# Attention output kept feature-major in a four-layer DiT stack: heads merged and sums gathered by DMA instead of TensorE transposes

## The chip, the cores and the metric

One Trainium2 chip, one core. The time is the device time of the kernel in microseconds (us), lower is better. TensorE is called PE, its weight loads PEld, VectorE DVE, ScalarE ACT, GpSimd POOL, and SyncE, whose queue issues most DMAs, SP.

## The reference

Sixteen sequences of 256 tokens with 256 features run through four layers, all in fp32. Of each attention block only this matters here (16 heads of 16 features):

```
def _attn(q, k, v):
    scores = jnp.einsum('bqhd,bkhd->bhqk', q, k) * scale
    w = jax.nn.softmax(scores, axis=-1)
    out = jnp.einsum('bhqk,bkhd->bqhd', w, v)
    return out.reshape(B, Lq, D_MODEL)
...
x = res + _attn(q, k, v) @ out_w          # self: 256 keys; cross: 77 context tokens
...
x = res + (gelu(xn @ ffn_w1.T + ffn_b1) @ ffn_w2.T + ffn_b2)
```

Layers L0, L2 and L3 are self attention, cross attention, MLP; L1 is cross attention alone. So a sequence passes 7 attention blocks and the kernel has 112 of them. L0's self attention also has a mask. Norms, modulation, gates, biases and rotary embedding differ from layer to layer and are not touched.

## The kernel before

A job is one sequence in one layer (64 jobs). Six jobs are in flight, each with its own slot of buffers. A job is cut into named steps, each on one engine. At build time a planner (`Program.run`) simulates the steps with a table of costs (`cost`), buffer rings and priorities, and writes down an order for each engine; at run time every engine goes through its own list in that order and waits on semaphores where a step's inputs or buffers are not there yet. So an engine whose next step must wait does nothing, even if a later step could run.

The steps of an attention block that are named below, with the line of their instructions:

- `qkv`: projections on PE (L1180, L1146). `ve` moves the values into `v_self` or `v_cross`, by ACT (L1426) or, where there is a bias, by DVE (L1617, L1625). There each head has 17 columns: its 16 features and a column of ones, so that the weighted sum also gives the softmax denominator.
- `S` (PE L1208 for self, L1222 for cross): a piece of the scores with queries in the partitions, written to one of two `score` banks. `mr` (DVE L1637) takes the row maxima out of that bank. `mx` (DVE L1650 to L1656) negates and turns them, and `sd` (SP, L1058) spreads them into `q_stack`. A self block has 8 `S`, a cross block 4.
- `ST` (PE L1238 for self, L1244 for cross): the same scores with keys in the partitions, less the maximum, into the same two banks. `ex` (ACT L1454) exponentiates them into `probs`.
- `W` (PE L1263): probabilities times values. Four heads sit in four 32-column tiles of the array. `pv` (ACT L1461) copies the sum of two `W` steps to `oT`: features of the heads in the partitions, tokens along the row. This is done in two halves of 8 heads.
- `oX` (PE L1274): four 128x128 transposes bring a half back to tokens in the partitions. `dv` (DVE L1665, L1666) inverts the sums and multiplies into `at`. `atT` (PE L1285): four transposes a block bring the result back to features in the partitions, `ae` (ACT L1466) copies it to `atT`, and `out` (PE L1146) projects it.

The MLP's steps are `up` (PE L1305), `ge` (ACT L1480) and `down` (PE L1314). The score steps use the array as row tiles of 64, `W` as column tiles of 32, all else as one tile.

## Time and profile before

| | |
|---|---|
| time, median of 3 runs | 2863.39 us (2859.39 to 2871.44) |
| profiled execution: first to last instruction | 2855.2 us |
| PE / DVE / ACT / POOL busy | 2716.6 / 1990.0 / 1433.3 / 290.6 us |
| mean granted TensorE clock | 0.973 of full |

The profiled execution has no other time of its own than its span, which is 8.2 us under the median of the runs and 4.2 us under the fastest; what lies around the span is in the runs' times. Busy time of PE counts each instruction from its first to its last moment, so neighbours overlap: what a group costs in a full stretch is read from the chain of waits, from its start to the next group's start. The layers lie one after another: L0 up to about 860 us, L1 to about 1200, then a passage, L2 from about 1400, L3 from about 1990 us.

### The profile page before, as it was taken

What the parts mean: (1) busy time and instruction counts of PE and PEld (TensorE: products, weight loads), DVE (VectorE), ACT (ScalarE), POOL (GpSimd) and SP (SyncE); (2) the same over time, 40 slices, a digit from 0 to 9 for tenths busy, and PEclk for the clock granted to TensorE, in tenths of its full rate; (3) what the DMA queues carried; (4) which work ended last, traced back from release to release, by engine and by line L of the source; (5) the groups of instructions that cost most, each with busy time, mean ns of one, the idle gap of its engine ahead of it and who ended that gap; (6) DMA issues with size and microseconds to landing.
All of it is one profiled execution on the core that took longest, in us unless ns stands there. A gap on an engine that the chain in (4) does not pass through costs nothing.

```text
span 2855.2 us, 57728 instructions
## 1 busy us (share of the span) xinstructions
PE 2716.6 (95%) x21118; PEld 2000.2 (70%) x21118; DVE 1990.0 (70%) x5348; ACT 1433.3 (50%) x2283; POOL 290.6 (10%) x346
## 2 busy tenths in 40 slices
PE   6989999999998999988999999999999999999998
PEld 5657777776766766665777777776777777676766
DVE  4677757766755577776777777776877777787751
ACT  1344554554455455444555555545555555555453
POOL 0000000000001111101111111110100000000000
PEclk9999999999999999997999999999999999999999
DMA  6443343343335366653434444434344433434320
GB/s 199 154 137 116 117 141 106 99 145 109 104 95 149 115 198 191 196 163 122 155 122 139 126 141 125 141 121 131 104 141 138 139 112 107 146 103 145 101 69 14
DMA packets 278894, 369.43 MB, mean 129 GB/s; under 512 B 31130, under 2 KB 157690, under 8 KB 278300
## 3 DMA queue, kind: packets, MB, share of 16 engines
q1 hardware_dynamic: 246172, 318.66, 36.8%
q10 hardware_dynamic: 32256, 47.07, 4.5%
q8 instruction: 177, 2.90, 0.4%
q14 instruction: 97, 0.79, 0.1%
q0 software_dynamic: 192, 0.01, 0.0%
HBM read 224.52 MB, written 110.97 MB: 118 GB/s over the span
## 4 chain that ended last, share of the span: by engine, by line
PE 70%; DVE 16%; issue 5%; DMA 4%; ACT 1%; SPq 1%; POOL 0%; ACTq 0%; DVEq 0%; POOLq 0%
PE gen L1305 11%; PE gen L1314 11%; PE gen L1180 10%; PE gen L1146 8%; PE gen L1263 8%; DVE row_max L1637 6%; PE score L1238 3%; PE score L1193 3%; PE score L1208 3%; PE score L1244 2%; PE gen L1274 2%; PE gen L1155 2%; PE score L1222 2%; DMA parts_scratch<-parts 2%; DVE maxT L1656 2%
## 5 line engine op out<-in xcount | busy, mean ns | idle before, releaser
L1637 DVE TENSOR_REDUCE row_max<-score 128x4 f32<-128x1024 f32 (+1 forms) x640 | 652.6, 1044 | 107.9 <-PE score L1222 88.2
L1454 ACT ACTIVATE probs<-score 128x1024 f32<-128x1024 f32 (+1 forms) x576 | 566.2, 1022 | 268.2 <-PE score L1238 170.3
L1305 PE MATMUL gen<-xnT,w_w1M 128*128 128x256 f32 x1536 | 378.4, 394 | 4.7 <-ACT xnT L1396 2.6
L1314 PE MATMUL gen<-w_w2M,hT 128*128 128x256 f32 x1536 | 354.8, 385 | 8.6 <-DVE x L1688 5.7
L1490 POOL TENSOR_TENSOR rstd<-var_eps,minus_half 128x2 f32<-128x2 f32 x160 | 111.5, 697 | 2175.1 <-DVE var_eps L1533 2175.1
L1314 PEld LDWEIGHTS gen<-w_w2M,hT 128*128 128x128 f32 x1536 | 286.2, 191 | 59.2 <-issue 22.3
L1305 PEld LDWEIGHTS gen<-xnT,w_w1M 128*128 128x128 f32 x1536 | 286.1, 194 | 58.8 <-issue 4.9
L1480 ACT ACTIVATE hT<-gen,b_b 128x256 f32<-128x256 f32 x384 | 160.2, 471 | 166.6 <-PE gen L1305 165.7
L1396 ACT ACTIVATE xnT<-gen,mod_all 128x256 f32<-128x256 f32 x288 | 147.0, 564 | 181.0 <-PE gen L1155 164.4
L1656 DVE STREAM_TRANSPOSE maxT<-max_tok 32x64 f32<-32x64 f32 x896 | 208.9, 233 | 17.1
L1461 ACT COPY oT<-gen 128x512 f32<-128x512 f32 x224 | 131.6, 587 | 171.4 <-PE gen L1263 168.9
L1208 PE MATMUL score<-k_self,q_stack 64*128 64x256 f32 x1536 | 195.7, 343 | 19.7 <-DVE row_max L1637 17.3
L1263 PE MATMUL gen<-probs,v_self 128*17 128x256 f32 x3072 | 201.8, 383 | 0.3 <-ACT probs L1454 0.3
L1686 DVE TENSOR_TENSOR xhat<-gen,gate 128x256 f32<-128x256 f32 (+1 forms) x112 | 60.2, 537 | 203.2 <-PE gen L1314 147.8
L1208 PEld LDWEIGHTS score<-k_self,q_stack 64*128 64x128 f32 x1536 | 128.1, 190 | 95.9 <-issue 77.0
L1238 PE MATMUL score<-q_stack,k_self 64*128 64x256 f32 x1536 | 181.2, 334 | 2.9 <-ACT probs L1454 2.2
L1222 PEld LDWEIGHTS score<-k_cross,q_stack 64*128 64x128 f32 x2048 | 137.5, 192 | 50.6 <-issue 49.5
L1238 PEld LDWEIGHTS score<-q_stack,k_self 64*128 64x128 f32 x1536 | 122.1, 188 | 64.5 <-issue 46.0
L1222 PE MATMUL score<-k_cross,q_stack 64*128 64x78 f32 x2048 | 156.3, 284 | 9.1 <-DVE row_max L1637 5.8
L1263 PE MATMUL gen<-probs,v_cross 77*17 77x256 f32 x2048 | 159.7, 402 | 4.9 <-DVE xhat L1666 1.9
L1665 DVE RECIPROCAL row_max<-gen 128x16 f32<-128x16 f32 x224 | 55.0, 246 | 133.1 <-PE gen L1274 132.9
L1274 PE MATMUL gen<-ident,oT 128*128 128x128 f32 x896 | 143.2, 284 | 0.0
(162 smaller groups left out, 4166.4 us busy)
## 6 DMA issues: line engine op xcount, KB each, us to landing
q_stack<-parts_scratch SPq DMA_DIRECT2D x336, 256.0 KB, 3.8
parts_scratch<-parts ACTq DMA_DIRECT2D x160, 256.0 KB, 2.6
parts_scratch<-parts SPq DMA_DIRECT2D x160, 256.0 KB, 2.9
k_self<-parts_scratch SPq DMA_DIRECT2D x144, 256.0 KB, 4.0
q_stack<-zeros_scratch SPq DMA_DIRECT2D x112, 256.0 KB, 3.9
q_stack<-maxT SPq DMA_DIRECT2D x224, 128.0 KB, 2.6
k_cross<-parts_scratch SPq DMA_DIRECT2D x192, 78.0 KB, 2.5
x_scratch<-x SPq DMA_DIRECT2D x48, 256.0 KB, 3.1
```

Source lines behind the costliest of these rows:

```text
L1146: mm = pe.matmul(out, xT[:, fc], weight[:, fc, cols], start=fc == 0, stop=fc == FC - 1)
L1180: mm = pe.matmul(out[:, c, :], weight[:, fc, cols], xT[:, fc, :], start=fc == 0, stop=fc == FC - 1)
L1208: mm = pe.matmul(buf[:, t, c * S:c * S + S], queries[rows, column(u), c * P:c * P + P], keys[rows, column(u), :], start=not blk.mask, stop ...
L1222: mm = pe.matmul(buf[:, t, at_col:at_col + CTXP], queries[rows, column(2 * u + i), c * P:c * P + P], keys[rows, column(2 * u + i), :], sta ...
L1238: mm = pe.matmul(buf[:, t, kc * S:kc * S + S], keys[rows, column(u), kc * P:kc * P + P], queries[rows, column(u), :], start=not blk.mask, ...
L1263: mm = pe.matmul(pv[VW * i:VW * i + VC, within, :], value, e, start=kc == 0, stop=not blk.whole or kc == TC - 1, skip_group_check=True)
L1274: mm = pe.transpose(buf[:, at_col:at_col + P], oT[before.buf][:, i, c * P:c * P + P], ident[:, :])
L1305: mm = pe.matmul(buf[:, i * S:i * S + S], w["M"]["w1"][:, fc, col:col + P], xnT[s][:, fc, :], start=fc == 0, stop=fc == FC - 1)
L1314: mm = pe.matmul(buf[:, 0:D], hT[:, j, c * P:c * P + P], w["M"]["w2"][:, j, :], start=j == 0, stop=j == FFC - 1)
L1454: act.activation(probs[st.probs][0:keys, :, :], score[st.fill.buf][0:keys, :, :].rearrange("p a (r q) -> p (a r) q", r=2), ACT.Exp, bias=k ...
L1637: dve.tensor_reduce(dst, src, AX_X, ALU.max).then_inc(max_done[b], 1)
L1656: ins = dve.transpose(maxT[st.got["max"]][:, :, 32 * b:32 * b + 32].bitcast(F32), max_tok[st.got["max"]][32 * b:32 * b + 32, :, :].bitcast ...
```

## The change

The attention output is no longer transposed. In `v_self` and `v_cross` two heads, one of each of two neighbouring groups, share 34 columns: a one, their features interleaved, a one. A `W` step takes 32 of the 34, so its tile holds the features of its own head in every second partition and the sum in the first or the last. `ve` needs two instructions where it had one. `pv` copies `oT` as before and one of the two groups also straight into `atT`. Two new SP steps follow each half: `sg` (2 DMAs) gathers the rows of sums into `sums`, `sh` (1 DMA) lays the other group's 64 partitions into `atT`. `dv`, now once a block, inverts the sums on DVE between two 32x32 block transposes, the second of which spreads each of them over its head's features; `nm` multiplies `atT` by the result. `oX`, `atT` and `ae` are gone with their three PSUM banks a block, and `out` waits for `nm`. The rows of the output weights are loaded in the interleaved order.

```
-VC = HD + 1
+VC = 2 * HD + 2
...
-            "ST": ..., "ex": 0.92, "W": ..., "pv": 0.48,
-            "oX": 0.44, "dv": 0.63, "atT": ..., "ae": ..., "out": 1.73,
+            "ST": ..., "ex": 0.92, "W": ..., "pv": 0.85,
+            "sg": 2.0, "sh": 2.1, "dv": 1.35, "nm": 0.63, "out": 1.73,
...
             pv = add("pv", h, "act", sums, sums[0])
-            oX = add("oX", h, "pe", [pv])
-            divided.append(add("dv", h, "dve", [oX], oX))
-        joined = []
-        for h in range(HALVES if blk.whole else 1):
-            atT = add("atT", h, "pe", divided[h:h + 1] if blk.whole else divided)
-            joined.append(add("ae", h, "act", [atT], atT))
-        out = add("out", 0, "pe", joined)
+            gathered.append(add("sg", h, "sp", [pv]))
+            placed.append(add("sh", h, "sp", [pv]))
+        scaled = add("nm", 0, "dve", [add("dv", 0, "dve", gathered)] + placed)
+        out = add("out", 0, "pe", [scaled])
...
+                def place_sums(st):
+                    s, h, buf = st.slot, st.j, of(st, "pv", st.j).buf
+                    sp.wait_ge(*moved(of(st, "pv", h).fill))
+                    sp.dma_start(sums[s][2 * h + 1:P:VW, 0, :], oT[buf][0:P:VW, 0, :]).then_inc(sums_placed[buf], 16)
+                    sp.dma_start(sums[s][2 * h:P:VW, 0, :], oT[buf][VW - 1:P:VW, 1, :]).then_inc(sums_placed[buf], 16)
+
+                def place_heads(st):
+                    ...
+                    sp.dma_start(atT[s][1:P:2, h, :], oT[buf][1:P:2, 0, :]).then_inc(heads_placed[buf], 16)
...
-                            mm = pe.matmul(pv[VW * i:VW * i + VC, within, :], value, e, start=kc == 0,
+                            mm = pe.matmul(pv[VW * i:VW * i + VW, within, :], value, e, start=kc == 0,
...
-                        act.copy(oT[st.buf][:, :, :], pv).then_inc(gen_moved[st.fill.buf], 1)
+                        act.copy(oT[st.buf][:, :, :], pv)
+                        act.copy(atT[s][:, j, :], pv[:, 1, :]).then_inc(gen_moved[st.fill.buf], 1)
...
+                def invert(st):
+                    s = st.slot
+                    for h in range(HALVES):
+                        dve.wait_ge(*sums_in(of(st, "sg", h)))
+                    link(dve.transpose(sums[s][:, 1, :], sums[s][:, 0, :]))
+                    total = rsum[s][:, :, :].rearrange("p c h -> p (c h)")
+                    link(dve.reciprocal(total.rearrange("p (h b e) -> p h b e", h=HALVES, e=2),
+                                        sums[s][:, 1, :].rearrange(...)[:, :, 0:2 * HALVES].rearrange(...)))
+                    link(dve.transpose(inverse[s][:, :, :].rearrange(...),
+                                       total.rearrange("p (n e) -> p n e", e=2).unsqueeze(2).to_broadcast([P, HALVES * S // VW, HD, 2])))
+
                 def divide(st):
...
+                    s = st.slot
+                    for h in range(HALVES):
+                        dve.wait_ge(*heads_in(of(st, "sh", h)))
+                    dve.tensor_tensor(atT[s][:, :, :], atT[s][:, :, :], inverse[s][:, :, :], ALU.mult).then_inc(divided, 1)
```

New steps and new costs give the planner's rules another order on every engine, not only around the removed steps. The first place is PE's list in L2, about the middle of the layer, where one sequence's `S` steps stand (one `S` is four matmuls `score<-k_self,q_stack`). Before:

```order
L1208 MATMUL score<-k_self,q_stack 128x256 x8
L1146 MATMUL gen<-w_outA,xnT 128x256 x4
L1208 MATMUL score<-k_self,q_stack 128x256 x4
L1305 MATMUL gen<-xnT,w_w1M 128x256 x4
L1208 MATMUL score<-k_self,q_stack 128x256 x4
L1305 MATMUL gen<-xnT,w_w1M 128x256 x4
L1208 MATMUL score<-k_self,q_stack 128x256 x4
L1305 MATMUL gen<-xnT,w_w1M 128x256 x4
L1208 MATMUL score<-k_self,q_stack 128x256 x4
L1305 MATMUL gen<-xnT,w_w1M 128x256 x4
L1146 MATMUL gen<-w_kvA,xnT 128x256 x4
L1244 MATMUL score<-q_stack,k_cross 77x256 x8
```

The same place of the changed kernel, with the same sequence's first `S` in the first row:

```order
L1238 MATMUL score<-k_self,q_stack 128x256 x4
L1176 MATMUL gen<-w_kvB,ctxT 77x256 x2
L1210 MATMUL gen<-xnT,w_qA 128x256 x4
L1238 MATMUL score<-k_self,q_stack 128x256 x28
L1274 MATMUL score<-q_stack,k_cross 77x256 x16
L1210 MATMUL gen<-xnT,w_kvA 128x256 x4
L1176 MATMUL gen<-w_outA,xnT 128x256 x4
```

The `up` steps (`gen<-xnT,w_w1M`) that stood between the `S` steps are elsewhere in the list, and seven `S` and four `ST` follow each other without anything between them.

The second place is DVE's list of the changed kernel at the same time: `mx` of another block, then the three instructions of `dv` (waiting for the gathered sums), two `mr`, another `mx`, `nm`, and the `mr` of the seven `S` steps above.

```order
L1663 STREAM_TRANSPOSE maxT<-max_tok 32x2x32 x4
L1672 STREAM_TRANSPOSE xhat<-xhat 128x256
L1674 RECIPROCAL row_max<-xhat 128x32
L1676 STREAM_TRANSPOSE xhat<-row_max 128x512
L1644 TENSOR_REDUCE row_max<-score 128x2x2x2
L1644 TENSOR_REDUCE row_max<-score 128x2x2
L1657 TENSOR_SCALAR max_tok<-row_max 128x4x4
L1659 SCALAR_TENSOR_TENSOR max_tok<-row_max,max_tok 128x2x4 x2
L1663 STREAM_TRANSPOSE maxT<-max_tok 32x2x32 x4
L1683 TENSOR_TENSOR xnT<-xnT,xhat 128x512
L1644 TENSOR_REDUCE row_max<-score 128x2x2 x7
```

Before, the two instructions of a `dv` (`row_max<-gen`, `xhat<-gen,row_max`) stood at such places, twice a block, and waited for PE:

```order
L1656 STREAM_TRANSPOSE maxT<-max_tok 32x2x32 x4
L1539 TENSOR_SCALAR xhat<-x,mean_var,rstd 128x256 x2
L1665 RECIPROCAL row_max<-gen 128x2x8
L1666 TENSOR_TENSOR xhat<-gen,row_max 128x2x128
L1637 TENSOR_REDUCE row_max<-score 128x2x2x2 x2
```

The third is SP's list of the changed kernel in the middle of the program, with the semaphores waited for: three halves' `sg` and `sh` (`xhat<-oT`, `xnT<-oT`) among the loads of the queries and keys. None of the `oT` rows was there before.

```order
L1011 DMA x_in<-x_scratch 128x2x256 [waits x_stored5,biased]
L1079 DMA xhat<-oT 4x256 [waits gen_moved3]
L1080 DMA xhat<-oT 4x256
L1079 DMA xhat<-oT 4x256 [waits gen_moved1]
L1080 DMA xhat<-oT 4x256
L1085 DMA xnT<-oT 64x256 [waits gen_moved3]
L1085 DMA xnT<-oT 64x256 [waits gen_moved1]
L1079 DMA xhat<-oT 4x256 [waits gen_moved3]
L1080 DMA xhat<-oT 4x256
L1085 DMA xnT<-oT 64x256 [waits gen_moved3]
L1047 DMA q_stack<-zeros_scratch 32x4x512 [waits score_full1]
```

Every SP row stands behind the ones above it, so the zeros for the next block's queries now also wait for three `pv`.

## Rows read from the trace of the kernel before

**Rows 1.** The page: busy us and share by engine; granted clock in 40 slices.

```profile
PE 2716.6 (95%) x21118; PEld 2000.2 (70%) x21118; DVE 1990.0 (70%) x5348; ACT 1433.3 (50%) x2283; POOL 290.6 (10%) x346
...
PEclk9999999999999999997999999999999999999999
```

**Rows 2.** The page: chain that ended last, shares of the span by engine.

```profile
PE 70%; DVE 16%; issue 5%; DMA 4%; ACT 1%; SPq 1%; POOL 0%; ACTq 0%; DVEq 0%; POOLq 0%
```

**Rows 3.** Windows by stage: length, busy us by engine, granted clock, DMA share, GB/s.

```profile
60.00:860.00 800.00, 766.85 (x6338) 555.57 (x6336) 546.82 (x1361) 385.53 (x581) 53.59 (x67) 0.98 0.39 122
...
1200.00:1400.00 200.00, 182.22 (x1370) 125.31 (x1369) 147.50 (x397) 93.20 (x151) 24.09 (x28) 0.86 0.47 146
1400.00:1990.00 590.00, 582.01 (x4532) 435.11 (x4530) 428.51 (x1151) 322.57 (x522) 91.59 (x104) 1.00 0.43 131
1990.00:2760.00 770.00, 749.08 (x5784) 557.53 (x5783) 589.05 (x1538) 424.28 (x664) 54.52 (x65) 1.00 0.39 120
```

**Rows 4.** Chain of waits in L2, 1500 to 1548 us: start, length, what.

```profile
1500.09 0.56 PE gen L1263 x8
1500.64 0.59 PE gen L1274 x4
...
1502.96 0.44 PE gen L1274 x4
...
1507.04 0.99 PE gen L1263 x16
...
1525.15 0.43 PE score L1208 x4
1525.58 1.92 PE gen L1305 x8
```

**Rows 5.** Groups by form, PE and PEld: busy us, mean ns, idle before.

```profile
L1305 PE MATMUL gen<-xnT,w_w1M 128*128 128x256 f32 x1536 | 378.4, 394 | 4.7 <-ACT xnT L1396 2.6 <-issue 2.1
...
L1274 PE MATMUL gen<-ident,oT 128*128 128x128 f32 x896 | 143.2, 284 | 0.0
...
L1285 PE MATMUL gen<-ident,xhat 128*128 128x128 f32 x448 | 81.1, 287 | 17.1 <-DVE xhat L1666 13.7 <-issue 2.4
...
L1305 PEld LDWEIGHTS gen<-xnT,w_w1M 128*128 128x128 f32 x1536 | 286.1, 194 | 58.8 <-issue 4.9 <-ACT xnT L1396 3.6
```

**Rows 6.** Groups by form, DVE: busy us, mean ns, idle before.

```profile
L1637 DVE TENSOR_REDUCE row_max<-score 128x4 f32<-128x1024 f32 x384 | 455.0, 1212 | 18.8 <-PE score L1208 18.3
...
L1656 DVE STREAM_TRANSPOSE maxT<-max_tok 32x64 f32<-32x64 f32 x896 | 208.9, 233 | 17.1
L1637 DVE TENSOR_REDUCE row_max<-score 128x8 f32<-128x616 f32 x256 | 198.0, 792 | 89.0 <-PE score L1222 88.2
...
L1666 DVE TENSOR_TENSOR xhat<-gen,row_max 128x256 f32<-128x256 f32 x224 | 95.1, 425 | 7.7
...
L1569 DVE STREAM_SHUFFLE parts<-gen 128x512 f32<-128x512 f32 x80 | 58.6, 732 | 0.4
L1574 DVE TENSOR_TENSOR turned<-turned,parts 128x512 f32<-128x512 f32 x80 | 55.4, 692 | 2.8
L1665 DVE RECIPROCAL row_max<-gen 128x16 f32<-128x16 f32 x224 | 55.0, 246 | 133.1 <-PE gen L1274 132.9
```

**Rows 7.** Groups by form, ACT: busy us, mean ns, idle before.

```profile
L1454 ACT ACTIVATE probs<-score 128x1024 f32<-128x1024 f32 x384 | 378.2, 1025 | 172.2 <-PE score L1238 170.3 <-PE gen L1263 0.9
...
L1461 ACT COPY oT<-gen 128x512 f32<-128x512 f32 x224 | 131.6, 587 | 171.4 <-PE gen L1263 168.9 <-ACT parts L1433 2.3
...
L1466 ACT COPY xnT<-gen 128x256 f32<-128x256 f32 x96 | 35.8, 373 | 63.9 <-PE gen L1285 63.8
```

**Rows 8.** Waits of PE: us in total, times, longest us.

```profile
PE score L1208 <- DVE row_max L1637: 17.3, 27, 2.0
```

**Rows 9.** Waits of SP's queue: us in total, times, longest us.

```profile
SPq L1058 <- DVE maxT L1656: 635.3, 204, 19.0
```

**Rows 10.** Line L1058, the spread of the maxima: issue to landing.

```profile
DMA to landing us min/median/max: 2.5/2.6/8.1
```

More of the change, by code:

```diff
@@ L163, in rings_of @@
     takes, gives = (), ()
-    if name in ("xT", "cT", "qkv", "oX", "atT", "out", "up", "down", "md", "mg"):
+    if name in ("xT", "cT", "qkv", "out", "up", "down", "md", "mg"):
         takes += ("gen",)
-    if name in ("xe", "ce", "ve", "rt", "dv", "ae", "res", "ge", "ma", "mh") or name == "lo" and not blk.rope:
+    if name in ("xe", "ce", "ve", "rt", "res", "ge", "ma", "mh") or name == "lo" and not blk.rope:
         gives += ("gen",)
@@ L217, in gives_needed @@
 def gives_needed(blk, ring):
-    return {"hid": TC, "parts": 2, "queries": blk.uses, "gates": TC if blk.kind == "mlp" else 1}.get(ring, 1)
+    return {"hid": TC, "parts": 2, "back": 2, "queries": blk.uses, "gates": TC if blk.kind == "mlp" else 1}.get(ring, 1)
 class Program:
@@ L499, in run @@
                 st.nth_way = seen[st.name, st.slot, "way", st.j, st.blk.whole or st.j == 0]
-def chunks_of(blk, h):
-    return [h] if blk.whole else list(range(FC))
 def column(n):
@@ L633, in weight_dmas @@
                     out.append((tiles["kv"][:, :, i * width:(i + 1) * width], src))
-                out.append((tiles["out"], wide[-1]))
+                out += out_rows(tiles["out"], a[names[-1]])
             for key, name in bias_loads.get((blk.of, blk.kind), {}).items():
@@ L840, in dit_stack @@
         xnT = per_slot("xnT", [P, FC, S])
-        at, delta, atT = xhat, xhat, xnT
+        sums, inverse, delta, atT = xhat, xhat, xhat, xnT
         ctx_in = [sb(f"ctx_in{i}", [CTX, D]) for i in range(CTX_IN)]
@@ L870, in dit_stack @@
         rows_ready = [slot_sems(f"rows_ready{h}_") for h in range(HALVES)]
+        sums_placed, heads_placed = ([sem(f"{n}{i}") for i in range(BACKS)] for n in ("sums_placed", "heads_placed"))
+        divided = sem("divided")
         biased = sem("biased")
@@ L1288, in project_out @@
                 def project_out(st):
                     s, blk = st.slot, st.blk
-                    for h in range(HALVES if blk.whole else 1):
-                        pe.wait_ge(*moved(of(st, "atT", h)))
+                    pe.wait_ge(divided, of(st, "nm").nth_all)
                     buf = fill(st)
@@ L1421, in _ @@
                             wait_own(st)
-                            src, out = gen[st.fill.buf][:, :].rearrange("p (c h d) -> p c h d", c=TC, h=H), v_self[own(st)][:, :, :, 0:HD]
+                            src, out = gen[st.fill.buf][:, :], v_self[own(st)][:, :, :, :].rearrange("p c n v -> p (c n) v")
                         else:
                             wait_cross(st)
-                            src, out = gen[st.fill.buf][0:CTX, 0:D].rearrange("p (h d) -> p h d", h=H), v_cross[cross_of(st)][:, :, 0:HD]
-                        act.copy(out, src).then_inc(gen_moved[st.fill.buf], 1)
+                            src, out = gen[st.fill.buf][0:CTX, 0:D], v_cross[cross_of(st)][:, :, :]
+                        for e in range(PER_HALF):
+                            ins = act.copy(interleaved(out, e), by_group(src, e))
+                        ins.then_inc(gen_moved[st.fill.buf], 1)
                     elif st.name == "ph":
```

103 lines of the change are left out of this document (48 added, 55 removed).

## Prediction

> **What bounds the kernel now.** I read the page first: PE is busy 95% of the span, DVE 70%, ACT 50% [rows 1]. The chain that ended last is PE for 70%, DVE for 16%, and DMA, issue and the rest for 14% [rows 2]: less work on PE is worth its full price in at most some 70% of the time. The stages differ [rows 3]. In L2 PE is busy 582 of 590 us at full clock, with DVE at 73%; in L3 749 of 770, with DVE at 76%; in L0 767 of 800; in the passage from L1 to L2 182 of 200, with the granted clock down to 0.86. So L2 is bound by PE alone, the rest nearly so. PE waits little for row maxima: 17.3 us in all at L1208 [rows 8], though a `mr` on a self block takes 1.212 us and the `S` that feeds it 0.43 [rows 4, 6]. That works because other PE work stands between the `S` steps (in [rows 4] a 1.92 us `up`).
>
> **The change part by part.**
>
> *Removed from PE.* 896 transposes in `oX` and 448 in `atT`, 1344 in all [rows 5]. Their mean of 284 ns overlaps; in a full stretch four take 0.44 us [rows 4]. 336 groups by 0.44 are **-148 us**. Their busy time, 143 + 81 = 224 us [rows 5], is the upper end. The Trainium skill (VectorE: DVE Perf Modes, The three transpose paths) gives 390 ns for a 128x128 transpose on TensorE; by that the change would remove 524 us, an estimate. The trace does not agree for transposes in a row (110 ns each), and the measurement decides. The same page's rules for kernel authors keep a 128x128 transpose on TensorE where the result may go to PSUM, which speaks against this change.
>
> *Tile shapes.* `oX` right behind a `W` takes 0.59 instead of 0.44 us, and 8 matmuls of a `W` 0.56 where 16 take 0.99 [rows 4]: a change of shape costs 0.07 to 0.15 us. In PE's list as written out there are 1787 such changes before and 1634 now. 153 by about 0.10 are **-16 us** (-10 to -23).
>
> *W with 32 columns for 17.* Eight matmuls cost 0.5 us, so four tiles together run as long as one full matmul (378.4 / 1536 = 0.246 us), and that one hides a load of all 128 columns [rows 4, 5]. Four tiles of 32 are 128 columns. Nothing.
>
> *What the new order gives back.* This is my main deduction. The freed PE time doesn't shorten DVE and ACT, and the list has changed: the `up` steps no longer stand between the `S` steps. There are two score banks, so from the third score step of an unbroken run on, PE goes at the pace of the reader: 1.212 us (self) or 0.792 (cross) for `mr`, 1.025 for `ex` [rows 6, 7]. I counted in PE's lists the runs of three or more score steps: 7 before, with 18 steps beyond the second; 40 now, with 146 (132 of them in L2 and L3; the longest run has 11 steps). More by 43 self `S` at 1.21 - 0.43 = 0.78 us: 34. More by 70 `ST` at 1.02 less their own length, for which I have 0.43 as an upper bound and take about 0.37: 45. More by 15 cross `S` at 0.3, between nothing and 0.79: 4. Together **+83 us**, nearly all in L2 and L3. The lower end is 0, if the readers are ahead whenever a run starts; the upper is 128 by 1.1, 140.
>
> *DVE inside the runs.* 39 more `mx` stand within runs than before; four of their small transposes alone are 4 by 0.233 = 0.93 us [rows 6]. `dv` and `nm` stand there too, as the order shows. At half of them PE has nothing else: **+20 us** (0 to 45).
>
> *DVE in total.* Gone: 224 by (0.246 + 0.425) = 150 us [rows 6]. New per block: a transpose of 128x512 like the shuffle of that size, 0.732; one of 128x256, between that and the 0.233 of 64 columns, on the line 0.45; a reciprocal of 32 columns, between 0.246 (16 columns) and twice that, 0.35; a 128x512 product, 0.692 [rows 6]. That is 2.22 us by 112 = 249. The 64 additions into the values, 0.425 us at the size 128x256, become two pieces each: between nothing and 27 us more. So DVE gains about 110 us and comes to 2100, 74% of the new span; it stays under PE. Where PE binds this is hidden; if DVE bound, it would be 110 us.
>
> *ACT.* `ae` goes (about 73 us: 96 by 0.373 and 64 by 0.587, the size of `oT`), a second `pv` copy of 128x256 comes (224 by 0.373 = 84) [rows 7], the split `ve` adds a few us. Near zero, on an engine at 50%.
>
> *The longer way to `out`.* Before, from the last `W`: `pv` 0.59, `oX` 0.6, `dv` 0.67, `atT` 0.4, `ae` 0.4, with five handovers of about 0.1, some 3.2 us. Now: 0.59 + 0.37 on ACT, SP issues two DMAs of at most 0.6 each, of which the nearest known one lands 2.6 us after its issue [rows 10], `dv` 1.53, `nm` 0.69: about 6.6 us. With six jobs in flight the full price, if the length of a job bound everywhere, is 112 by 3.4 / 6 = 63 us. PE's list has other work between the last `W` and `out`, an estimate from the lengths of such steps is 7 us in L1 and 11 to 23 in L2, so only L1 and part of L0 are tight: **+20 us** (0 to 63).
>
> *SP and the DMA queues.* 672 more DMAs, 16.5 MB in 16,000 pieces of 1 KB. SP goes through its list in order and already stands 635 us at the spread of the maxima [rows 9]. Taken as hidden; priced among the rivals. `oX` and `atT` also held PSUM banks; fewer takers can only help.
>
> Sum on the profiled execution: 2855 - 148 - 16 + 83 + 20 + 20 = **2814 us**. The median of the runs lies 8 us over the span: **2822 us**.
>
> **The rivals.**
>
> 1. *As above: part of the PE time comes back at runs of score steps*, 2822, its own range 2775 to 2865. Chance 0.50. For it: the counts, and DVE at 73 to 76% in L2 and L3 before its 110 us more. Below 2849 in 0.38, within 0.5% in 0.12.
> 2. *All of it is collected.* PE stays at 95% because its list has work whenever a reader is late: 2855 - 148 - 16 + 20 = 2711, with 8 more 2719. Against it: the order quoted, where 11 score steps follow each other. Up to 2775 counts here. Chance 0.16.
> 3. *TensorE's clock falls where PE now waits.* In the passage after L1 the granted clock is 0.86 where PE had gaps; in L2, without gaps, 1.00 [rows 3]. If L2 and L3 got 0.93, halfway, their 1331 us of PE work less some 75 for the transposes would take 7% longer, +90 us at most: 2870 to 2912. The Trainium skill (TensorE: Matmul & The Clock Gate, HAM oscillation) has such a rule: gaps in PE's work bring the half clock back; the stages here agree with it. But the waits in a run are under 1 us each, like those in L0, where the clock is 0.98. This is the rival on the slower side; it decides from a mean clock of about 0.95 in L2 and L3, 5% of 1256 us = 63 us, which with the sum passes 2878. Chance 0.15: 0.13 slower, 0.02 within.
> 4. *DVE or SP stand in their lists behind the gathered sums.* `dv` waits for DMAs that need `pv`, ACT, SP's place and a landing of 2.5 to 8.1 us [rows 10]; `mr` is queued behind it, and PE waits for `mr`. And 58 of the 224 `sd` now stand right behind an `sh`, so the maxima wait for another block's `pv`. At 1 us for each of 112 blocks: 2822 + 112 = 2934; from 0.5 us it is over 2878. Chance 0.12: 0.09 slower, 0.03 within.
> 5. *The transposes were free anyway*, filling gaps, and nothing changes: 2863. Against it PE's 98.6% in L2 [rows 3]. Chance 0.07, within.
>
> **How the numbers follow.** About 0.5% (14 us) is what a measurement of this kernel can tell from no change. Faster: 0.38 + 0.16 = 0.54. Same: 0.12 + 0.02 + 0.03 + 0.07 = 0.24. Slower: 0.13 + 0.09 = 0.22. The range for 8 in 10 leaves out the lower half of case 2 and the dearer halves of 3 and 4: 2735 to 2895. That the change does what it says is in the order; there no rival is needed.
>
> **What would show each step.** Right: 1344 fewer PE matmuls; PE busy down by 148 to 224 us and its share of the span from 95% to near 90%; PE's wait for row maxima at the self `S` up from 17.3 us [rows 8] to 50 or more, with a like wait for `ex` at `ST`, in L2 and L3; L2 hardly shorter (its 590 us) while L0 gives back about 35 us; DVE busy near 2100; the second transpose of `dv` near 0.73 us; granted clock still about 0.97. Wrong: DVE waiting tens of us for `xhat<-oT` DMAs (rival 4), `out` waiting for `nm` by more than 60 us in total (the longer way mis-sized), a clock under 0.95 in L2 (rival 3), or L2 at 555 us with PE at 98% (rival 2). The prediction fails most easily at the +83: it prices runs by their list alone, and not by who is ahead when one starts.

## The result: 5.3% slower, and the profile after

The changed kernel takes 3012.7 us (median, 3010.8 to 3026.4) against 2862.8 for the kernel before on the same chip, a ratio of 1.053 (1.050 to 1.056). The forecast was 2822, with a range of 2735 to 2895. The profiled execution spans 3009.3 us, 154 more than before.

The page of the changed kernel: busy time by engine, the granted clock in 40 slices, and the chain's shares by engine.

```profile
PE 2729.1 (91%) x19774; PEld 1968.5 (65%) x19774; DVE 2091.7 (70%) x5412; ACT 1500.5 (50%) x2469; POOL 294.6 (10%) x346
...
PEclk9889999999999888888989998988899998899999
...
PE 51%; DVE 27%; issue 7%; DMA 5%; ACT 5%; SPq 3%; POOL 0%; ACTq 0%; DVEq 0%; POOLq 0%
```

Beside [rows 1, 2]: PE's busy time has grown by 12 us although 1344 of its matmuls are gone, its share fell from 95 to 91%, and of the chain it now holds 51% where it held 70; DVE went from 16 to 27%, ACT from 1 to 5, SP's queue from 1 to 3. The clock row shows an 8 in 13 of the 27 slices behind L0; before, one slice had a 7 and all others a 9.

The windows by stage, as [rows 3] (length, busy us of PE, PEld, DVE, ACT, POOL, clock, DMA share, GB/s; the layers now end at other times, so the rows serve for rates only):

```profile
60.00:860.00 800.00, 743.48 (x5940) 526.98 (x5939) 564.49 (x1353) 415.44 (x642) 54.17 (x67) 0.95 0.41 126
1200.00:1400.00 200.00, 176.27 (x1266) 117.62 (x1264) 153.93 (x411) 89.56 (x151) 24.25 (x29) 0.84 0.49 157
1400.00:1990.00 590.00, 533.95 (x3820) 388.74 (x3818) 417.34 (x1090) 298.07 (x484) 83.87 (x95) 0.91 0.40 125
1990.00:2760.00 770.00, 694.34 (x4790) 503.12 (x4786) 552.80 (x1368) 391.68 (x644) 55.79 (x64) 0.90 0.38 119
```

L2 ran at full clock with PE at 98.6%; now the same window has PE at 90.5% and clock 0.91, and the one behind it 90.2% and 0.90. By the starts of every sixteenth store the layers took 1003, 367, 773 and 709 us before, and 992, 390, 850 and 775 now: L0 gained 11, L2 and L3 lost 143.

Span, busy time and mean clock divide the loss into three. Idle is the span less PE's busy time; the clock's part is busy time by (1 - clock); the work is busy time by clock.

| us | before | after | moved | predicted |
|---|---|---|---|---|
| PE work at full clock | 2643 | 2494 | -149 | -164 |
| PE idle | 139 | 280 | +142 | +123 |
| lost to TensorE's clock (0.973, 0.914) | 73 | 235 | +161 | 0 |
| span | 2855 | 3009 | +154 | -41 |

The removal and the giving back came out within 20 us each. The third row was missing from the sum.

The three parts add up to the span by construction, so they do not say by themselves that each us was on the path. The trace gives a check: the clock was at its half level in 20 stretches of 157 us in all before and in 60 stretches of 516 us after. The chain that ended last spends 122 us of those on PE before and 362 after, which would be half as long at full clock. So 61 and 181 us of the clock's part lie on the chain, 120 of the 161 added; the rest stands where another engine set the pace. One more limit: the profiled execution of the kernel before (2855) is 4 us shorter than the fastest of its timed runs and 8 shorter than their median, so differences to it are good to some 10 us.

Waits of the changed kernel: us in total, times, longest.

```profile
DVE xhat L1672 <- DMA xhat<-oT: 124.3, 48, 12.3
...
PE score L1238 <- DVE row_max L1644: 65.9, 73, 4.9
...
PE score L1223 <- DVE row_max L1644: 29.2, 39, 2.5
PE score L1274 <- DVE row_max L1644: 27.7, 47, 3.4
...
PE gen L1176 <- DVE xnT L1683: 19.7, 12, 3.8
```

PE's wait for row maxima at the self `S` went from 17.3 us [rows 8] to 65.9, as forecast. Over all score steps the same view gives 41 us before and 144 after, and for `ex` (`ACT probs`) 7 and 33. By the trace an `mr` was running for 112 us of those 144 (32 of the 41 before), and `dv`, `nm` and `mx` for 21. The first row is the mark that the prediction had set for rival 4: DVE stands 124 us at `dv` until the gathered sums land. But PE's waits for row maxima rarely follow: 17 us of them fall into a DVE wait for the sums or the 5 us behind it. `out` waits for `nm` 20 us on PE, and 30 at its weight loads.

SP's queue, same columns:

```profile
SPq L1073 <- DVE maxT L1663: 480.9, 160, 10.9
SPq L1079 <- ACT xnT L1471: 273.0, 111, 11.0
```

The `sg` now stand 273 us for `pv`. The maxima's own wait is shorter than in [rows 9] (480.9 for 635.3), but that is no gain: SP comes to them later. It waited at 160 of the 224 `sd` where it had waited at 204, so at 64 of them the maxima stood ready. From the end of the last transpose of `mx` to the start of its `sd` the trace has 89 us in all, 23 before.

Five windows of 10 us in L2 of the changed kernel, columns as above, and then the chain of waits there:

```profile
2120.00:2130.00 10.00, 10.00 (x63) 7.84 (x61) 6.27 (x12) 5.92 (x9) 0.00 (x0) 1.00 0.58 190
2130.00:2140.00 10.00, 10.00 (x77) 8.04 (x76) 8.03 (x21) 1.38 (x3) 0.00 (x0) 1.00 0.71 219
2140.00:2150.00 10.00, 6.70 (x40) 3.95 (x38) 9.89 (x15) 1.41 (x5) 0.00 (x0) 0.76 0.30 93
2150.00:2160.00 10.00, 9.51 (x56) 5.29 (x56) 6.38 (x26) 5.32 (x7) 2.68 (x3) 0.56 0.14 35
2160.00:2170.00 10.00, 10.00 (x99) 7.33 (x97) 7.56 (x27) 9.50 (x17) 1.39 (x2) 1.00 0.26 78
```

```profile
2142.38 6.65 DVE row_max L1644 x6
...
2149.08 1.21 DVE row_max L1644
...
2150.43 0.71 PE score L1274 x4
...
2153.56 1.86 PE gen L1294 x16
2155.43 3.60 PE gen L1176 x8
...
2163.14 1.00 PE gen L1294 x16
```

This is one run of score steps: the chain goes through six `mr` and then a seventh. PE writes a bank in 0.43 us [rows 4] and stands until `mr` has read the other one, 1.2 us a piece. In the third window PE is idle for 3.3 us, in spells of 0.33 to 0.96, and its mean clock is 0.76; in the fourth it is 0.56. The half level was granted from 2145.1 us on, behind idle spells of 0.96 and 0.63 us, and the full one again from 2158.8, after PE had worked without a gap from 2150.4. In the fourth window PE is busy 95% again, but everything takes about twice its time: 16 matmuls of `W` 1.86 us and eight full ones 3.60, where [rows 4] has 0.99 and 1.92. By busy time and clock the two windows have 6.70 x 0.24 + 9.51 x 0.44 = 1.6 + 4.2 us of lost clock, and 3.8 us of idle time. The 1.6 cost nothing: up to 2150.43 the chain is the `mr`, and a slower `S` only shortens PE's stall. The 4.2 are on PE's own part of the chain.

The Trainium skill (TensorE: Matmul & The Clock Gate, A second HAM failure mode: psum-queue depth-cycling) tells of a bf16 kernel in which short idle spells between groups of matmuls were frequent enough for the clock to swing between its two levels. The trace agrees for fp32: spells of 0.33 to 0.96 us stand around the fall at 2145.1.

A second place, 1744 to 1752 us, the chain:

```profile
1744.43 0.55 SPq L1079
1745.02 3.59 DMA xhat<-oT
...
1748.70 0.46 DVE xhat L1672
1749.18 0.36 DVE row_max L1674
1749.57 0.72 DVE xhat L1676
1750.36 1.10 issue
1751.46 1.22 DVE row_max L1644
```

SP's issue, the landing of the sums, `dv`, and only then the `mr`: the new way stands in front of row maxima. PE had written both banks by 1749.0 us and the next `mr` began at 1750.3; PE then stood for 0.74 us, and in the run behind it for four more spells of 0.42 to 1.97. Such places exist, but by the 17 us named above they are few. Around 1726 to 1731 us the chain takes the same way (a landing of 1.56 us), and PE is busy without a gap there.

DVE's and ACT's new groups, as [rows 6, 7]:

```profile
L1676 DVE STREAM_TRANSPOSE xhat<-row_max 128x512 f32<-128x512 f32 x112 | 79.7, 711 | 3.9
...
L1683 DVE TENSOR_TENSOR xnT<-xnT,xhat 128x512 f32<-128x512 f32 x112 | 76.7, 687 | 5.3 <-DMA xnT<-oT 3.9
...
L1672 DVE STREAM_TRANSPOSE xhat<-xhat 128x256 f32<-128x256 f32 x112 | 49.5, 442 | 125.5 <-DMA xhat<-oT 124.3
...
L1674 DVE RECIPROCAL row_max<-xhat 128x32 f32<-128x32 f32 x112 | 39.5, 353 | 3.8
```

```profile
L1485 ACT ACT_TABLE_LOAD x81 | 103.9, 1283 | 63.6 <-PE gen L1314 61.7 <-ACT parts L1440 0.4 <-issue 0.3
L1461 ACT ACT_TABLE_LOAD x80 | 102.6, 1283 | 2.7 <-ACT parts L1453 0.5 <-ACT parts L1440 0.4 <-PE gen L1294 0.4
L1471 ACT COPY xnT<-gen 128x256 f32<-128x256 f32 x224 | 87.1, 389 | 0.0
```

The durations were forecast well: 442, 353, 711 and 687 ns for 0.45, 0.35, 0.732 and 0.692 us, the second `pv` copy 389 for 373. DVE comes to 2092 us for 2100. ACT did not stay at its time: 1433 before, 1500 now. The loads of activation tables, 1.283 us each, went from 104 to 162: 74 us that come from the new order, in which `ge` and `ex` alternate more often.

### The profile page after: what moved, and what is told of

Same layout as the page of the kernel before. It is cut to its first block, busy times and chain, and to the rows that moved or that the text cites. A ratio compares the mean times of both kernels' runs of the same rounds, so it can differ in the third digit from the quotient of the medians.

```text
span 3009.3 us, 55877 instructions
## 1 busy us (share of the span) xinstructions
PE 2729.1 (91%) x19774; PEld 1968.5 (65%) x19774; DVE 2091.7 (70%) x5412; ACT 1500.5 (50%) x2469; POOL 294.6 (10%) x346
## 4 chain that ended last, share of the span: by engine, by line
PE 51%; DVE 27%; issue 7%; DMA 5%; ACT 5%; SPq 3%; POOL 0%; ACTq 0%; DVEq 0%; POOLq 0%
DVE row_max L1644 11%; PE gen L1314 8%; PE gen L1210 8%; PE gen L1323 8%; PE gen L1294 7%; PE gen L1176 6%; PE score L1268 3%; DVE maxT L1663 3%; PE score L1252 2%; PE score L1223 2%; PE gen L1185 2%; DMA parts_scratch<-parts 2%; DMA xhat<-oT 2%; ACT probs L1461 2%; PE score L1274 2%
## 5 line engine op out<-in xcount | busy, mean ns | idle before, releaser
L1314 PE MATMUL gen<-xnT,w_w1M 128*128 128x256 f32 x1536 | 360.5, 387 | 3.0 <-ACT xnT L1401 2.2
L1238 PE MATMUL score<-k_self,q_stack 64*128 64x256 f32 x1536 | 205.5, 355 | 68.9 <-DVE row_max L1644 65.9
L1294 PE MATMUL gen<-probs,v_self 128*32 128x256 f32 x3072 | 215.7, 402 | 2.2 <-DVE parts L1603 1.4
L1268 PE MATMUL score<-q_stack,k_self 64*128 64x256 f32 x1536 | 195.5, 349 | 19.0 <-ACT probs L1461 13.2
L1252 PEld LDWEIGHTS score<-k_cross,q_stack 64*128 64x128 f32 x2048 | 150.8, 209 | 72.6 <-issue 72.0
L1252 PE MATMUL score<-k_cross,q_stack 64*128 64x78 f32 x2048 | 171.9, 303 | 20.5 <-DVE row_max L1644 16.2
L1294 PE MATMUL gen<-probs,v_cross 77*32 77x256 f32 x2048 | 172.4, 427 | 5.6 <-ACT probs L1461 3.3
L1702 DVE TENSOR_TENSOR xhat<-gen,gate 128x512 f32<-128x512 f32 (+1 forms) x112 | 60.2, 538 | 148.6 <-PE gen L1323 100.0
L1274 PE MATMUL score<-q_stack,k_cross 64*77 64x256 f32 x1024 | 123.8, 337 | 42.5 <-DVE row_max L1644 27.7
L1451 ACT ACTIVATE parts<-gen,b_qk 128x256 fp32r<-128x256 f32 (+1 forms) x192 | 71.0, 426 | 149.9 <-PE gen L1210 126.7
```

The costliest lines, as they stand in the source:

```text
L1238: mm = pe.matmul(buf[:, t, c * S:c * S + S], queries[rows, column(u), c * P:c * P + P], keys[rows, column(u), :], start=not blk.mask, stop ...
L1252: mm = pe.matmul(buf[:, t, at_col:at_col + CTXP], queries[rows, column(2 * u + i), c * P:c * P + P], keys[rows, column(2 * u + i), :], sta ...
L1268: mm = pe.matmul(buf[:, t, kc * S:kc * S + S], keys[rows, column(u), kc * P:kc * P + P], queries[rows, column(u), :], start=not blk.mask, ...
L1274: mm = pe.matmul(buf[0:CTX, t, i * S:i * S + S], keys[rows, column(2 * u + i), 0:CTX], queries[rows, column(2 * u + i), :], start=True, st ...
L1294: mm = pe.matmul(pv[VW * i:VW * i + VW, within, :], value, e, start=kc == 0, stop=not blk.whole or kc == TC - 1, skip_group_check=True)
L1314: mm = pe.matmul(buf[:, i * S:i * S + S], w["M"]["w1"][:, fc, col:col + P], xnT[s][:, fc, :], start=fc == 0, stop=fc == FC - 1)
```

## The experiments

Three theories. **Order**: the list that the planner wrote for the new graph, out of costs that are too short, opens gaps on PE, and the clock doubles their price. **Path**: the new instructions and DMAs cost it by themselves, whatever the list. **DVE**: its 102 us more are the loss. A ratio is to the kernel before on the same chip, with its 95% interval.

**1. Before, with three of four transposes left out.** In `transpose_back` and `transpose_output`:

```
-for c in range(TC): for i in range(PER_HALF):
+for c in range(1): for i in range(1):
...
-for i, fc in enumerate(chunks): for c in range(TC):
+for i, fc in enumerate(chunks[:1]): for c in range(1):
```

> The kernel before with its own order and every wait, but each oX and atT issues one transpose and not all four (or two), so the attention output is not computed right. This is the removal of PE work alone: about 1008 of the 1344 transposes, some 111 us of PE work. Theory A (the new waits and TensorE's clock did the harm, and the removal itself is good): the span falls by 50 to 110 us, to 2750 to 2810, unless the gaps that the removal opens already pull the clock down. Theory B (in this kernel any gap on PE costs more than it saves, because the clock falls to half in and behind it): the span stays within 30 us of 2855 or rises, and the half-clock time goes up from 158 us. Theory C (the transposes were free): no change and no change of the clock.

2843.3 us, 0.992 (0.991 to 0.994). PE work at full clock fell by 92 us (2643 to 2551), and the kernel got only 22 us faster (0.8%): idle time rose by 39 and the clock's part by 42. (The three parts give 11 us for the profiled pair of executions, the medians 22.) This is what theory B expected: within 30 us, with more half clock. So in the old list, with nothing added, this work of PE is worth a quarter of its size at most. What a list made for the shorter steps would collect, this run does not show.

**2. The changed kernel without the gathering of the sums.** `place_sums` is empty, and the waits for it on ACT and DVE are gone.

```
-sp.dma_start(sums[s][2 * h + 1:P:VW, 0, :], ...).then_inc(sums_placed[buf], 16)
-sp.dma_start(sums[s][2 * h:P:VW, 0, :], ...).then_inc(sums_placed[buf], 16)
...
-act.wait_ge(*sums_in(of(before, "sg", before.j)))
...
-for h in range(HALVES): dve.wait_ge(*sums_in(of(st, "sg", h)))
```

> The changed kernel with its order kept, but without the two DMAs that gather the sums and without the wait for them on DVE and ACT: dv inverts whatever stands in the tile, so the division is not by the softmax sums. DVE's 124 us of waiting for the sums and SP's 273 us of standing at sg ahead of other transfers (partly kept at sh) are gone. Theory A1 (in-order waits for the gathered sums start the gaps): the time falls from 3012 by 80 us or more, to 2930 or less, and the clock rises from 0.914 to 0.94 or more. Theory A2 (the gaps come from the list's runs of score steps, which stay): under 40 us, clock about 0.92.

2965.0 us, 1.035 (1.033 to 1.037). The whole DMA way of the sums, waits included, is worth 48 us of the 150, between the 80 and more of A1 and the less than 40 of A2. PE's idle time fell by 10 us, as did its wait for row maxima (144 to 134), and the clock's part by 39. So DVE's 124 us at the sums show in PE's idle time by 10 us only; why the clock answered with 39 is not shown.

**3. The changed kernel with more work on PE.** The first four matmuls of every `W` run twice.

```
-for kc in range(TC if blk.whole else 1):
+for kc in [0] + list(range(TC if blk.whole else 1)):
```

> The changed kernel with more PE work and nothing else: the first four matmuls of every W are issued twice, the second time over the first, 1792 matmuls, about 112 us of PE work at full clock. The result is unchanged. Theory B (the clock is the loss): the time rises by clearly less than 112 us, or falls, since work fills slack and keeps the clock up; mean clock over 0.93. If the clock does not answer to such work: plus 60 to 112 us and the clock still 0.91.

3109.8 us, 1.085 (1.083 to 1.088), 97 more than the changed kernel. PE work at full clock rose by 184 us (2494 to 2678); the 448 repeated groups of four, eight matmul records each in the trace, are 0.41 us each, not the 0.25 behind the 112 us that I expected; [rows 4] has 0.56 us for eight records of `W`. Idle time fell by 46, the clock's part by 46 as well. Half the added work was free, and half of what was free came from the clock: filling gaps brings the clock back as opening them takes it.

**4. The changed kernel, planned with longer durations.** Nothing but the numbers in `ISSUE` and `cost` (values alone, first the old, then the new):

```
-"ln": 1.14, "mr": 1.13 / 0.71, "mx": 0.92, "pv": 0.85, "sg": 2.0 (issue 0.86), "sh": 2.1, "dv": 1.35, "nm": 0.63
+"ln": 1.3,  "mr": 1.24 / 0.82, "mx": 1.45, "pv": 0.98, "sg": 3.3 (issue 1.1),  "sh": 2.6, "dv": 1.6,  "nm": 0.72
```

> The changed kernel with its instructions, but the planner's cost table as this trace shows the steps: sg 3.3 and sh 2.6 us to landing, dv 1.6, nm 0.72, pv 0.98, mx 1.45, mr 1.24 and 0.82, ln 1.3, SP time of sg 1.1. Only the order changes. Theory A1/A2 (the order, made with too short costs, puts DVE at the sums too early and mr in runs): 2880 to 2960 us, DVE's wait for the sums under 60 us, clock above 0.93. Theory D (the new path and DVE load cannot be hidden whatever the order): within 30 us of 3012.

2910.1 us, 1.017 (1.014 to 1.020): the same steps and DMAs in another order are 103 us faster. PE's wait for row maxima fell from 144 us to 64. Its wait for the sums:

```profile
DVE xhat L1672 <- DMA xhat<-oT: 85.3, 30, 10.4
```

That wait stayed above the 60 us expected. Most of the new entries are near lengths that the trace shows, but not the 3.3 us of `sg`: by the semaphore events in the trace of the changed kernel, the time from the issue of the first of its two DMAs to the last landing is 2.3 us at the median, 2.7 in the mean and 6.6 at most. Which of the entries brought the 103 us was not tried apart.

**5. Before, planned with the same `ln`, `mr` and `mx`.**

> The kernel before with the same instructions in number and kind; only three costs of the planner's table are set to what the traces show (mr 1.24 and 0.82, mx 1.45, ln 1.3 us), as in e4, so every engine gets another order. It asks how much an order alone moves the time, and whether the better costs are good in themselves. Theory O (the order of the kernel before is a good one by tuning, and any other graph or cost gives a worse one): slower by 1 to 4%, 2890 to 2980, with more gaps on PE than 120 us and a clock under 0.96. Theory P (measured costs are simply better, and e4's gain is theirs): faster than 2865 by 10 us or more.

2879.8 us, 1.005 (1.004 to 1.007), less than the 1 to 4% of theory O and no gain as P had it. These three entries do not help the old graph, so number 4 is not a gain that both would have; `pv`, `sg`, `sh`, `dv` and `nm`, changed in number 4 too, have no counterpart here.

**6, 7 and 8. Other weights in the rule that picks a step.** The rule takes the least of 12 x job - rank - 4 if the step keeps PE's tile shape.

```
-min(can, key=lambda st: (12 * st.job - st.rank - 4 * (...), 0))
+min(can, key=lambda st: (10 * st.job - st.rank - 5 * (...), 0))     # 6, the kernel of number 4
+min(can, key=lambda st: (12 * st.job - st.rank - 0 * (...), 0))     # 7, the kernel of number 4
+min(can, key=lambda st: (10 * st.job - st.rank - 0.5 * (...), 0))   # 8, the kernel of number 5
```

> e4 (the changed kernel, measured costs), with two weights of the planner's choice altered: a job's age counts 10 and not 12, staying in a tile shape 5 and not 4. Only the order differs from e4. Theory O (what the change is worth is decided by the order that it gets): this order moves the time by 1% or more from e4's 2910, and by the planner's own count, which puts it shorter, down: 2830 to 2890. If the new path's own work and waits were the loss, it stays within 15 us of 2910.

> e4 with the bonus for staying in a tile shape taken away (0 and not 4): 31 runs of three or more score steps with 100 steps beyond the second, against 38 with 105 in e4, and 122 activation table loads against 158. Theory R (runs of score steps and table loads decide): 2860 to 2900. More changes of tile shape cost PE work, at about 0.1 us each. Theory O alone allows 2850 to 2930.

> e5 (the kernel before, measured costs) with weights 10 for age and 0.5 for the tile shape: the fair partner of e6, the planner's best order for the graph of before by the same costs. Theory O: between 2850 and 2920, so that before and after, each with a fresh order, lie within 2% of each other and below the 5% measured; if the new path is itself bad, this one beats e6 by 50 us or more.

Number 6: 2879.6 us, 1.005 (1.003 to 1.008). Number 7: 2915.8 us, 1.017 (1.012 to 1.022). Number 8: 2893.8 us, 1.012 (1.008 to 1.017). The changed graph under four lists takes 3013, 2910, 2880 and 2916 us; the old one under three 2863, 2880 and 2894. The best of the lists that I made for each come to the same 2880; the old graph's own list remains 17 us better than both. So the order accounts for up to 133 of the 150 us, and a difference of 20 us between two kernels of this kind says nothing of their instructions. PE's wait for row maxima is 54 us in number 6 and 65 in number 7.

Number 7 missed its 2860 to 2900. It has fewer runs of score steps than number 4 (31 with 100 steps beyond the second, for 38 with 105) and 122 table loads for 158, and is no faster; number 6, with 39 runs and 111 steps, is the faster one. So neither count ranks the lists.

**9. Number 6 with the sums planned later** (6.0 us for `sg`, weights 12 and 5).

> The changed kernel, output complete, with the measured costs, the step that gathers the sums entered at 6.0 us where 3.3 was measured (so that the planner puts dv later in DVE's list), and the planner's weights 12 and 5. Theory (what is lost now are waits in order, and their echo in TensorE's clock): DVE's wait for the gathered sums falls from 74 us (weights 10 and 5) to under 30, PE's idle time falls from about 180 to 160 us, and the time is 2840 to 2870. Rival (DVE's wait for the sums is no longer on the path, it only stands where DVE would wait anyway): the wait falls but the time stays at 2870 to 2900, by the luck of the new list.

2880.5 us, 1.004 (1.001 to 1.006). Of number 6 and of this kernel the row of the wait for the sums, in this order:

```profile
DVE xhat L1672 <- DMA xhat<-oT: 74.2, 29, 8.7
```

```profile
DVE xhat L1672 <- DMA xhat<-oT: 18.1, 7, 7.7
```

The wait is down from 74 to 18 us and the time is the same, as the rival said; PE's idle time did not fall as the theory had it (207 us for 199). The list is another one throughout, so this alone does not show the wait to be free; number 11 keeps the list.

**10. Before, with the first row maximum of each block taken twice.**

```
+if u == 0: link(dve.tensor_reduce(dst, src, AX_X, ALU.max))
 dve.tensor_reduce(dst, src, AX_X, ALU.max).then_inc(max_done[b], 1)
```

> The kernel before, output complete, same list on every engine; the first row maximum of each attention block is taken twice (48 of 1.21 us and 64 of 0.79, about 109 us more DVE work; the changed kernel has 102 more). Theory (the order, not the work on DVE, made the loss): 2863 becomes 2890 to 2930, since some of the repeats hold up a bank that PE waits for; DVE busy about 2100; PE's idle time grows by 20 to 50 us, and what the clock takes grows by about as much. Rival (a DVE that is about 105 us longer is what costs the changed kernel its 150 us, whatever the order): 2970 or more. Rival (DVE's work is hidden behind PE): 2863 to 2875.

2943.8 us, 1.026 (1.022 to 1.029). The page's busy row, the two groups added and the waits behind them:

```profile
PE 2753.3 (94%) x21118; PEld 2019.8 (69%) x21118; DVE 2096.2 (71%) x5460; ACT 1436.7 (49%) x2283; POOL 290.9 (10%) x346
```

```profile
L1638 DVE TENSOR_REDUCE row_max<-score 128x4 f32<-128x1024 f32 x48 | 57.4, 1196 | 10.3 <-PE score L1208 10.2
...
L1638 DVE TENSOR_REDUCE row_max<-score 128x8 f32<-128x616 f32 x64 | 50.9, 795 | 40.8 <-PE score L1222 40.0
```

```profile
PE score L1208 <- DVE row_max L1639: 39.6, 47, 3.1
...
PE score L1193 <- DVE row_max L1639: 20.6, 23, 3.3
```

108 us more on DVE cost 78 us in the old list, above the 2890 to 2930 expected and below the rival's 2970: the wait at the self `S` went from 17.3 to 39.6 us, that at all score steps from 41 to 87, idle time rose by 49 and the clock's part by 32. DVE at 70% is not cover. Each of these repeats holds a score bank, so 0.7 us a us is a price for work in front of a row maximum, not for any work on DVE.

**11. Number 6 without the gathering of the sums** (the edit of number 2).

> The changed kernel in the order of measured costs with weights 10 and 5 (2880 us), without the two DMAs a half that gather the softmax sums and without the waits for them, so that the division uses other numbers (that part of the computation is left out). Theory (the 74 us for which DVE waits for the sums still hold up row maxima): 2840 to 2860, PE's idle time 20 us less and the clock's part less by as much. Rival (that wait is idle time that DVE has to spare): 2875 to 2880. In the changed kernel as given the same edit took 48 us off 3013, where DVE waited 124 us.

2839.4 us, 0.992 (0.988 to 0.997), 40 less than number 6 in the same list. So the sums' way as a whole still costs 40 us. That is not DVE's wait alone: the edit takes 448 DMAs and SP's waits for `pv` in front of them. PE's idle time fell by 20 us, of which 8 are waits for row maxima (54 to 46) and 8 waits for DMAs (26 to 18), and the `sd` start 98 us late in all where number 6 has 163. In number 6 only 4 of PE's 54 us fall into a DVE wait for the sums or the 5 us behind it. The theory's numbers were met or nearly so (2840 to 2860, 20 us less idle time, as much less for the clock); that it is DVE's wait was not shown.

**12. The product on POOL.** Weights 12 and 4, 6.0 us for `sg`, 1.4 for `nm`.

```
-scaled = add("nm", 0, "dve", ...)
+scaled = add("nm", 0, "pool", ...)
...
+pool.wait_ge(inverted, of(st, "dv").nth_all)
...
+pool.tensor_tensor(atT[s][:, :, :], atT[s][:, :, :], inverse[s][:, :, :], ALU.mult).then_inc(divided, 1)
```

> The changed kernel, output complete, with the measured costs, the sums' step entered at 6.0 us, weights 12 and 4, and the product nm (0.69 us on DVE, 112 times, 77 us) on POOL, which does a sum of the same size in 1.3 us and is idle for 90% of the span. Theory (work on DVE costs this kernel about 0.7 us a us, as the repeated maxima showed on the kernel before: 78 us for 106): DVE busy about 2015, and 2880 becomes 2820 to 2845, below the kernel before. Rival (the repeated maxima were dear only because each held a score bank, and DVE's other work is hidden behind PE): 2865 to 2885. Rival (POOL's product is 0.6 us longer, ends later, and its work in SBUF slows DVE's): over 2890, with DVE's groups longer per instruction.

2861.5 us, 0.999 (0.997 to 1.001). The busy row, and the new group on POOL:

```profile
PE 2658.7 (93%) x19774; PEld 1900.3 (67%) x19774; DVE 2032.1 (71%) x5300; ACT 1431.0 (50%) x2417; POOL 436.4 (15%) x458
```

```profile
L1504 POOL TENSOR_TENSOR xnT<-xnT,xhat 128x512 f32<-128x512 f32 x112 | 143.2, 1278 | 1249.0 <-DVE xhat L1682 1142.9 <-DMA xnT<-oT 106.1
```

DVE is 60 us shorter than in number 9 and the kernel 19 us faster, between the theory's 35 to 60 and the rival's nothing; the list differs too (28 runs of score steps with 74 beyond the second, for 35 with 97). It is the best of the changed graph with its whole computation, and it equals the kernel before. The Trainium skill (SBUF — State Buffer, Summary: rules for kernel authors) warns that a DVE instruction with two SBUF inputs and a GpSimd one that reads SBUF block each other. At 1278 ns the product takes no longer than the sums of the same size that POOL did anyway. The trace agrees that DVE is held up, in an instruction of `mx` with two SBUF inputs. Its row in number 9 and then in this kernel:

```profile
L1659 DVE SCALAR_TENSOR_TENSOR max_tok<-row_max,max_tok 128x8 fp32r<-128x8 f32 x448 | 60.1, 175 | 7.8 <-DVE max_tok L1657 0.2
```

```profile
L1665 DVE SCALAR_TENSOR_TENSOR max_tok<-row_max,max_tok 128x8 fp32r<-128x8 f32 x448 | 76.6, 212 | 7.9 <-DVE max_tok L1663 0.2
```

The 30 of them that overlap a product took 716 ns in the mean and up to 1289, the other 418 took 176. That is some 16 us more on DVE, against the 77 us taken off it.

All profiled executions, divided as above, in us:

| kernel | span | PE work | idle | clock |
|---|---|---|---|---|
| before | 2855 | 2643 | 139 | 73 |
| after | 3009 | 2494 | 280 | 235 |
| 1 fewer transposes | 2844 | 2551 | 178 | 115 |
| 2 no sums | 2960 | 2493 | 270 | 196 |
| 3 `W` repeated | 3101 | 2678 | 234 | 189 |
| 4 longer costs | 2904 | 2506 | 221 | 177 |
| 5 before, longer costs | 2879 | 2624 | 143 | 112 |
| 6 weights 10, 5 | 2872 | 2516 | 199 | 158 |
| 7 weights 12, 0 | 2924 | 2517 | 229 | 178 |
| 8 before, 10, 0.5 | 2889 | 2667 | 134 | 88 |
| 9 late sums | 2873 | 2512 | 207 | 155 |
| 10 before, more DVE | 2942 | 2649 | 188 | 105 |
| 11 = 6, no sums | 2833 | 2513 | 179 | 141 |
| 12 product on POOL | 2857 | 2518 | 198 | 141 |

The kernels of the changed graph, number 3 aside, have 125 to 150 us less work for PE than the kernel before, and give it back in the two last columns: all of it and more in most, just all of it in number 12, 108 of 130 in number 11. Where idle time rises by 39 us or more over the kernel before, the clock's part rises with it, by 0.65 (number 10) to 1.7 (number 11) us for each. It is no function of idle time alone: number 5 has 4 us more of it and loses 39 to the clock. The work column is not exact either: the same instructions of the graph before give 2624, 2643 and 2667 us in three lists.

## Why the prediction was wrong

- **The step that failed** is the zero for the clock in the sum, with rival 3 kept apart from it. The prediction said "the waits in a run are under 1 us each, like those in L0, where the clock is 0.98" and priced the clock as an alternative, at 0.15. The waits were under 1 us for the most part, as said (0.33 to 0.96 in the windows shown), and the clock fell all the same. It is not an alternative: numbers 1, 3 and 10 each change PE's idle time in an unchanged list, and the clock's part goes with it (+39 and +42, -46 and -46, +49 and +32 us); so it does in number 11 against number 6 (-20 and -17), while in number 2 it moved more than the idle time (-10 and -39). So rivals 1 and 3 are one case. The measured +142 came with +161, of which 120 lie on the chain. The threshold I had set for it, a mean clock of 0.95 in L2 and L3, was passed (0.91 and 0.90). With the price of number 3, one us of clock for one of idle, my own sum would have been 2822 + 123 = 2945, still 68 us short.
- **Removed from PE, tile shapes:** -164 forecast, -149 measured at full clock. Right in size, as far as the work column tells 20 us apart. But the working took them at full price on a path of which PE had 70%; number 1 shows at most a quarter of such work arriving in the old list.
- **Runs of score steps, DVE inside them, longer way:** +123 forecast, +142 measured as idle time, with waits where they were forecast (65.9 us at the self `S`); by the gaps between PE's instructions 109 of the 141 us added lie in L2 and L3. By PE's waits the runs were right in sum and wrong in their parts: the pace of `mr` took 80 us more where 38 were forecast, `ex` 26 where 45 were. Other DVE work in PE's waits for maxima (`mx`, `dv`, `nm` and the rest) took 25 more, 20 forecast; at `out` stood 20, as forecast. Rival 4 had its sign, DVE's 124 us at the sums, but only 17 us of PE's waits stand near one; the sums' whole way cost 48 us (number 2).
- **DVE in total "hidden":** wrong for whatever stands in front of a row maximum; number 10 prices that at 0.7 us a us.
- **ACT near zero:** wrong by 67 us of busy time, 74 us more of table loads. They come with the order, which I had read for PE, DVE and SP and not for ACT: 162 loads in the changed kernel, 110 in number 12, 104 before. What they cost was not tried apart.
- **`W` with 32 columns for nothing:** right. 16 matmuls take 1.00 us in full stretches of the changed kernel, 0.99 before [rows 4].
- **SP "hidden":** not quite. The `sd` start 66 us later in all than before, counted from their maxima. The landing of `sh` is short (1.9 us where 2.6 was the nearest row). The 40 to 48 us of numbers 11 and 2 are the price of the sums' whole way; how much of it is DVE's place in its list, and how much SP's queue, was not separated.
- **What decides it:** the order. The kernel as given was planned with entries that are too short (`mx` 0.92 us, `dv` 1.35 for 1.5, `sg` 2.0 for 2.3 at the median). Longer ones and other weights bring 3013 to 2880 without touching an instruction, and PE's wait for row maxima from 144 us to 54, near the 41 of before.

Open: why one list is 30 us better than another with nearly the same costs (numbers 6 and 7). Also open: why number 5 has hardly more idle time than the kernel before and loses 39 us more to the clock. A list of the changed graph that beats the kernel before was not found: 125 us less work for PE end in the same time at best, since idle time and clock take them back.

## What to carry to other kernels

Work taken off the busiest engine is worth its size only if its list stays free of gaps; leave the work out first (number 1) and see what arrives before building its replacement. Do not price gaps on TensorE and a falling clock as alternatives: in this kernel each us of new idle time came with 0.65 to 1.7 us lost to the clock, of which a part is hidden where PE waits for another engine anyway. Where a planner orders the kernel, check its entries for the new steps against a trace before judging the new steps, and compare each graph's best list with the other's. A long wait of an engine in front of its input (DVE's 124 us) need not be a wait of the engine that bounds: look at what that one waits for.

## What the runs showed of the hardware

- TensorE's granted clock was 0.76 and 0.56 in two windows of 10 us around a run of idle spells of 0.33 to 0.96 us, with PE busy 67% and 95%. In the windows beside them, with PE busy 100%, it was 1.00.
- A DMA between SBUF tiles of 64 KB, 64 partitions by 1 KB, lands 1.9 us after its issue at the median, 5.6 at most; SP needs 0.52 us to issue it. Without the sums' DMAs in front of it the median was 2.7 (number 2) and 2.6 (number 11); why was not tried. The row of the changed kernel's line L1085:

```profile
DMA to landing us min/median/max: 1.8/1.9/5.6
```

- A 32x32 block transpose on DVE takes 442 ns for 256 fp32 columns and 711 for 512, the latter with a source that repeats each column pair sixteen times.
- A product of two 128x512 fp32 tiles takes 1278 ns on POOL and 687 on DVE.
- A small DVE instruction with two SBUF inputs (128x8) took 716 ns in the mean, 1289 at most, where it overlapped the product on POOL, and 176 where it did not (number 12).
